# Second layer of a two-layer kernel: a second buffer for the odd decays, and the Silu one pair later with the next even decay pulled in front of the scaling

## The reference

```
xz = group_norm(x) @ in_proj_w.T ; xv, z = split(xz)
xc = silu(depthwise_conv3x3(xv) + conv_b)               # 256 inner channels
xs = four orders of the pixels of two windows, L = 128   # k = 0..3, two of them backwards
dt, B, C = x_proj(xs) ; dt = softplus(dt_proj(dt) + bias)
for l in range(L):                                       # 16 states n for each channel
    h = h * exp(dt[l] * A[n]) + (dt * u)[l] * B[n, l]
    y[l] = sum over n of h * C[n, l]
out = x + (layernorm(sum of the four orders of (y + D * xs)) * silu(z)) @ out_proj_w.T
```

## Time and profile before

| what | value |
|---|---|
| median of 3 runs | 27614.51 us (27614.04 to 27621.61) |
| profiled execution: own time, span | 27622.95 us, 27621.2 us |
| DVE busy | 25285.8 us (92%) |
| ACT busy | 23632.0 us (86%) |
| POOL busy | 23358.9 us (85%) |
| PE busy | 21957.3 us (79%) |
| 16 DMA engines, queue q1 | 33.0% |

### The profile page before, as it was taken

How to read it: one execution, slowest core, us unless ns; L and a number is a source line. 1 busy time by engine, 2 the same in 40 slices (tenths; PEclk the granted TensorE clock), 3 DMA queues, 4 the chain that set the end, 5 groups by cost and what they waited for, 6 DMA issues and landing times.

```text
span 27621.2 us, 494663 instructions
## 1 busy us (share of the span) xinstructions
PE 21957.3 (79%) x145198; PEld 16882.3 (61%) x145198; DVE 25285.8 (92%) x23743; ACT 23632.0 (86%) x48522; POOL 23358.9 (85%) x10372
## 2 busy tenths in 40 slices
PE   5888588788887888887888888888788888888887
PEld 1666366666666666666666666666666666666666
DVE  7777599999999999999999999999999999999998
ACT  2677488988989988889898898888898998888988
POOL 4000399999999999999999999999999999999999
PEclk6999799999999999999999999999999999999999
DMA  4111433333333333333333333333333333333333
GB/s 148 48 46 46 150 105 106 107 105 107 106 107 107 107 106 107 106 107 105 107 106 106 106 108 105 108 104 108 105 107 105 108 104 108 106 106 107 106 107 97
DMA packets 2189148, 2868.62 MB, mean 104 GB/s; under 512 B 695002, under 2 KB 964858, under 8 KB 2177786
## 3 DMA queue, kind: packets, MB, share of 16 engines
q1 hardware_dynamic: 2181978, 2803.33, 33.0%
q10 hardware_dynamic: 4608, 33.82, 0.3%
HBM read 2667.01 MB, written 169.74 MB: 103 GB/s over the span
## 4 chain that ended last, share of the span: by engine, by line
ACT 28%; PE 25%; issue 18%; DVE 12%; POOL 4%; ACTq 1%; DVEq 1%; DMA 0%; SPq 0%; POOLq 0%
DVE hst L1530 11%; PE yps L1240 7%; ACT dbT L1420 6%; ACT dA L1398 6%; ACT dAs L1398 6%; PE dbx L1225 5%; PE misc L1140 5%; POOL hc L1607 2%; POOL dbu L1593 2%; DVE hc L1538 2%; ACT vab L1353 1%; PE misc L1159 1%; PE misc L1176 1%; PE cps L1216 1%; ACT vab L1339 1%
## 5 line engine op out<-in xcount | busy, mean ns | idle before, releaser
L1593 POOL TENSOR_TENSOR dbu<-dtu,bb 128x1024 f32<-128x1024 f32 x4096 | 9697.6, 2374 | 1209.2 <-DVE hst L1530 1208.3
L1530 DVE TENSOR_TENSOR_SCAN hst<-dA,dbu 128x1024 f32<-128x1024 f32 x4096 | 9336.8, 2279 | 778.1 <-ACT dA L1398 755.9
L1607 POOL TENSOR_TENSOR hc<-hst,cc 128x1024 f32<-128x1024 f32 x4096 | 9743.1, 2379 | 5.6 <-DVE hst L1530 3.7
L1240 PE MATMUL yps<-ident,hc 128*128 128x128 f32 x65536 | 8944.2, 283 | 328.6 <-POOL hc L1607 325.1
L1240 PEld LDWEIGHTS yps<-ident,hc 128*128 128x128 f32 x65536 | 7982.1, 147 | 1824.7 <-issue 1273.4
L1530 DVE TENSOR_TENSOR_SCAN hst<-dAs,dbx 128x1024 f32<-128x1024 f32 x3584 | 8104.2, 2261 | 63.5 <-issue 61.2
L1225 PE MATMUL dbx<-ident,dbT 128*128 128x128 f32 x28672 | 4153.0, 292 | 3329.9 <-DVE hst L1530 2975.1
L1225 PEld LDWEIGHTS dbx<-ident,dbT 128*128 128x128 f32 x28672 | 3391.2, 148 | 4750.2 <-DVE hst L1530 3639.0
L1420 ACT ACTIVATE dbT<-dtuT,bT 128x256 f32<-128x256 f32 x14336 | 6125.1, 495 | 18.2
L1398 ACT ACTIVATE dA<-dtv,aneg 128x508 f32<-128x508 f32 x8192 | 5291.6, 678 | 400.0 <-DVE hst L1530 396.1
L1398 ACT ACTIVATE dAs<-dtv,aneg 128x508 f32<-128x508 f32 x7168 | 4743.7, 710 | 531.0 <-DVE hst L1530 528.8
(11 more groups left out here) (187 smaller groups left out, 25145.4 us busy)
## 6 DMA issues: line engine op xcount, KB each, us to landing
bb<-l_bscr SPq DMA_DIRECT2D x1024, 1024.0 KB, 5.7
cc<-l_bscr SPq DMA_DIRECT2D x1024, 1024.0 KB, 5.5
bx<-l_bscr SPq DMA_DIRECT2D x1024, 256.0 KB, 6.1
xg<-xgp SPq DMA_DIRECT2D x512, 85.0 KB, 2.5
xgp<-xb ACTq DMA_DIRECT2D x32, 1032.0 KB, 9.4
xt<-in_x_dram SPq DMA_DIRECT2D x128, 256.0 KB, 2.7
l_xnT<-xo SPq DMA_DIRECT2D x128, 256.0 KB, 2.0
xn<-l_xnT SPq DMA_DIRECT2D x256, 128.0 KB, 2.1
```

The costliest lines, as they stand in the source:

```text
L1240: mm = pe.matmul(yps[:, p, f * P:(f + 1) * P], hc[:, u % HB, f * 512 + p * P:f * 512 + (p + 1) * P], ident[:], is_transpose=True, start=fi ...
L1530: nc.vector.tensor_tensor_scan(hst[:, v % 4, way], decays.rearrange("p f c -> p (f c)")[:, way], inputs.rearrange("p f c -> p (f c)")[:, way],
L1593: nc.gpsimd.tensor_tensor(to, dtu[:, step % 2], row.unsqueeze(1).to_broadcast([P, 2, 512]), ALU.mult).then_inc(s_inp, 1)
L1607: nc.gpsimd.tensor_tensor(hc[:, v % HB].rearrange("p (f c) -> p f c", f=2), hst[:, v % 4].rearrange("p (f c) -> p f c", f=2), row.unsqueez ...
```

## The change

The second layer's odd decays alternate between the two halves of dAs by v // 2 % 2, and no longer by the direction of the step. The decay of a turned unit then waits for scan(v - 4), the last reader of its half, and the zero column is written anew at states 1 and 3 of each step, once for each half. silus moves from u = 40 to u = 42, and decay(46), which was the first thing of the pair u = 44, is issued right behind it, ahead of scale(47), the side copy of unit 42 and the take of that pair. The initial clearing of dAs is dropped.

```
-                    nc.vector.memset(dAs[:], 0.0)
...
-        DS_AT, LN_AT, GATED_AT, SILU_AT = (7, 8, 9, 10), 12, 39, 40
+        DS_AT, LN_AT, GATED_AT, SILU_AT = (7, 8, 9, 10), 12, 39, 42
...
-                    wait(act, s_scan, b * UN + (v - 1))
                     if turned(v):
-                        out = dAs[:, step % 2].rearrange("p f (s l) -> p f s l", l=P)
+                        wait(act, s_scan, b * UN + (v - 3))
+                        out = dAs[:, v // 2 % 2].rearrange("p f (s l) -> p f s l", l=P)
                     else:
+                        wait(act, s_scan, b * UN + (v - 1))
                         out = (dbx if v % 2 else dA).rearrange("p f (s l) -> p f s l", l=P)
                     lo, hi = (0, P - 1) if back else (1, P)
-                    if st == 0 or st in PLAIN_ODD:
+                    if st in (0, 1, 3) or st in PLAIN_ODD:
...
                         if u + 2 < UN:
-                            decay(ph, u + 2, b)
+                            if u != SILU_AT + 2:
+                                decay(ph, u + 2, b)
...
                         if u == SILU_AT:
                             silus(ph, not last, True, b)
+                            decay(ph, u + 4, b)
...
-                        decays, inputs = dAs[:, step % 2], dbx
+                        decays, inputs = dAs[:, v // 2 % 2], dbx
```

## The result

The changed kernel takes 28173.04 us (median of 4; 28172.54 to 28186.49), against 27615.59 us before in the same rounds. The ratio is 1.0202, with a 95% interval of 1.0185 to 1.0218: 2.0% slower, 557 us. The direction was forecast, the size was not: the forecast was 27961 us and the range ended at 28130.

The account below looks back on a forecast made before the run. No engine full; DVE, the fullest, bound by waits for even decays (755.9 us) and C rows (312.0 us). Loss 2.3 + 0.25 + 0.16 = 2.7 us a block, x 128 = 347 us: 27961 us, range 27800 to 28130.

Parts of the forecast that it names:

- The main term: At hc(44): a 3.17 us stall at scan(44) goes, one of about 5.5 us comes; loss 2.3 us a block.
- The drain: At silus's table loads: the skill page's drain would add 2.8 us, making the loss 5.1 us a block; left out.
- PE's clock: At spread(44): after over 4 us idle, PE runs it at the low clock; 0.25 us more a block.
- slower still: Rival at hc(46): the pair behind the stall is 1.2 us late too; 3.9 us a block, 28113 us; chance 0.23.
- The buffers: Odd decays: two buffers end ACT's 528.8 us of waits, gain zero; added zero columns cost 0.16 us a block at decay(19).
- the 2.10 us ahead of
scan(20): Sign at scan(20): its late decay's 2.10 us wait stays, because ACT there waits for PE's convolution.
- The pulled decay: Decay(46) behind silus, ahead of scale(47): adds 1.22 us on ACT's way to the side copy and hc(44).

Follow-up runs that it names:

- PE kept busy: The changed kernel plus 40 unused transposes of the identity on PE after total(42), before the wait for the side copy; 27917.00 us, 1.0110 of the kernel before.
- the pull at 40: The kernel before with silus left at unit 40 and decay(44) issued right behind it, ahead of scale(45); 27724.93 us, ratio 1.0037.
- the last: Kernel before with decay(44) ahead of scale(45), silus at 40, plus unused PE transposes: 24 at unit 41, 24 after unit 57, 18 at block head; 28383.72 us.

## Why the prediction was right or wrong

**The main term held.** Decay(46) to side copy to spread to hc(44) came as worked out, step by step: silus starts 1.35 us after decay(45) and ends at the expected distance, with 4.62 us from the first table load to decay(46) (10165.77 to 10170.39). The intervals from scan(43) and from scan(45) sum to -3.27 + 5.93 = 2.66 us a block; the forecast for them was 2.3 + 0.25. The drain that the Trainium skill ("ScalarE: Activation LUTs", What ACT_TABLE_LOAD costs) adds to a table load isn't there in this trace either.

**The step that failed** is the term "PE's clock", taken at 0.25 us a block for the spread alone. That much was right of the spread: with PE kept busy, the interval that holds hc(44) is 0.19 us shorter. But the block is 2.26 us shorter, 1.76 of them behind silus, 1.19 of these at hc(46) and scan(48). I had counted the loss up to hc(44) and let everything behind it move along unchanged. But PE's next pair ran at the 1.2 GHz level for its first 3 us and some more, with the side copy of unit 44 late for it, and decay(48) behind that: +1.24 us from scan(47) to scan(48). That chain stood among the rivals, as "slower still", with 1.2 us and 28113 us; its reason "against" (the low clock lasts only some 3 us) was no reason, because 3 us hold a spread, a job, a fill and most of a total, and here it lasted some 4 us from the end of PE's wait. That rival had the mechanism, and 0.23 of the chances. Its sum still falls 60 us short; neither had the 0.42 us from scan(52) to scan(53) (54 us) nor the smaller shifts far from silus, which cancel in part, such as +0.26 us at scan(3) and -0.38 at scan(11). For what PE does after such a wait, the rule of the Trainium skill ("TensorE: Matmul & The Clock Gate", Part 1) agrees with the trace: two levels, the low one after the idle time (0.50 behind the wait of 5.64 us, 1.00 from 10179).

**The buffers.** Taken at no gain: right, the run with them alone shows none, and the 2.10 us ahead of scan(20) are still there (2.11 in the changed kernel). Their cost was put at 0.16 us a block at decay(19). The interval from scan(19) to scan(20) changed by 0.01 us; where a cost shows is scan(53), in the crowded stretch behind silus. In two settings they cost nothing that can be told from noise (27648 against 27623, and 27728 against 27725 with the pulled decay), in a third 127 us (28099 against 27971). Of these 127 us, 60 are the interval at scan(3), where fewer blocks had the full clock (23 against 64), and 27 the one at scan(52). That the two zero columns behind silus make the 0.21 us at scan(53) is argued from their 0.10 us each, not shown.

**The pulled decay.** I priced it as its own 1.2 us on the way to hc(44), and that is its effect at hc(44) (5.79 against 4.55 us). Over the block it costs 74 us in the full change, 102 at 40 and 296 with the side copy between the Silus. Around silus the three are alike: 0.77, 0.80 and 0.93 us a block; what makes the times differ so much is elsewhere in the block, in the last case 1.04 us at scan(3). I had not seen that scale ahead of the decay is what keeps PE fed; my expectation for the pull at 40 repeated that error.

**Was the copy the cause?** It was the releaser of the largest wait. Removing it from behind silus took 5.4 us off that wait, and 0.77 us a block off the intervals around silus (0.92 without the pull), which in the times were 33 and 255 us. A wait names what came last, and behind it other late work was queued, nearly as late. What costs is 4.6 us of ACT in a pair that has a side copy for PE as well as the decay and the scaling, and PE's idle time that comes with it. How the 445 us for the move divide between ACT's lateness and the clock can't be given as a sum, since each hides part of the other; with the clock kept up, 294 us over the kernel before remain (27917 against 27623).

**Left open.** It is open why a kernel has the full clock at the head of few or of many blocks, and why the packets of instructions come late where they do. The first alone makes up to 1.3 us a block between two of these kernels (+0.40 with the side copy between the Silus, -0.92 in the last), 169 us or 0.6%, far from any edit. So a difference of that size says little of the edit by itself; its intervals do.

## What to carry to other kernels

When a long piece of work is moved on an in-order queue, list everything behind it up to the point where the queue has caught up again, and not only the first instruction that another engine waits for; then price the engine that was left idle as slow, for its whole next piece of work. A wait that is removed from an engine which is late through others moves to its next wait: 529 us of ACT's waits went away here and no time with them. The largest wait in the profile names a gate, and not what it is worth; open it and measure the next one before building on it. And compare two kernels interval by interval before crediting the edit with the whole difference: here the same edit, the copy moved between the Silus, read as 33 us in one setting and 255 in another, and as 0.8 and 0.9 us a block where it acts.

## What the runs showed of the hardware

An unused filling of 40 matmuls made the changed kernel 0.9% faster. TensorE then left its wait at the full clock: the fill behind it took 1.04 us in place of 1.91. The same trick elsewhere did the opposite: with 18 more matmuls near the head of the loop over blocks, and 24 at unit 57, PE stood for 399 us in waits named issue, and with 24 more at unit 41 for 754 us, up to 9.4 us at a time. The kernel with 28 added at unit 41 alone had 189 us of such waits, at the head of the block and not at the added instructions. In each of these kernels the loop takes one more packet of instructions in queue q8 for each pass (1406 against 1280), and PE goes on some 1.4 us after such a packet has ended. So added instructions of PE can cost time many units away. The number of added matmuls alone doesn't decide it: with 40 there were 24 packets more and no such wait. That q8 is PE's queue is my reading, from these starts and from its count, which grew in each kernel with added matmuls and in no other.
